# First pass of the attention maximum on 48 rows as two row tiles of the array, with query and key parts stored once

## What is computed

```python
q = shape((xn @ Wq + bq) * SCALING)            # [B*H, L, D], float32
k = shape(xn @ Wk + bk)
attn_weights = einsum('btd,bsd->bts', q, k) + _rel_to_abs(einsum('btd,md->btm', q, rel_k[0]))
attn_probs = softmax(attn_weights, axis=-1)
attn_output = einsum('bts,bsd->btd', attn_probs, v) + einsum('btm,md->btd', _abs_to_rel(attn_probs), rel_v[0])
...
x = x + out_projection(attn_output) + top-2 of 8 experts (xn)
```

## Time and profile before

| | before |
|---|---|
| median of 3 runs | 2135.35 us (2133.4 to 2136.01) |
| the profiled execution, its time | 2129.37 us |
| its span in the profile | 2127.8 us |
| projection and routing | 0 to 194.7 us |
| first pass of group 0, with 8 relative windows | 194.7 to 298 us |
| groups of attention | 298 to about 1190 us |
| experts and combination | about 1190 to 2127.8 us |
| PE, DVE, ACT, POOL busy | 84%, 73%, 51%, 27% |

### The profile page before, as it was taken

How to read it: one execution, slowest core, us unless ns; L and a number is a source line. 1 busy time by engine, 2 the same in 40 slices (tenths; PEclk the granted TensorE clock), 3 DMA queues, 4 the chain that set the end, 5 groups by cost and what they waited for, 6 DMA issues and landing times. The chain is left out here.

```text
span 2127.8 us, 36339 instructions
## 1 busy us (share of the span) xinstructions
PE 1782.1 (84%) x11121; PEld 1025.8 (48%) x11121; DVE 1559.4 (73%) x2621; ACT 1092.2 (51%) x2076; POOL 564.5 (27%) x414
## 2 busy tenths in 40 slices
PE   6992339999999989999888599999999999999920
PEld 4762002333333322333222277777777777788820
DVE  3764787788888878877653298888888888885523
ACT  2541006666666666666878544445444444455500
POOL 1002454233333333300000133323232323320046
PEclk9995559999999999999999799999999999999965
DMA  5998994454444544434551475766666666756535
GB/s 181 341 345 280 261 292 137 123 132 121 134 133 131 137 136 134 114 69 109 161 165 60 173 244 210 250 218 232 219 234 231 222 246 212 253 169 202 168 99 148
DMA packets 214446, 394.97 MB, mean 186 GB/s; under 512 B 16080, under 2 KB 144096, under 8 KB 206176
## 3 DMA queue, kind: packets, MB, share of 16 engines
q1 hardware_dynamic: 189232, 275.33, 42.5%
q0 software_dynamic: 20784, 101.99, 13.9%
q10 hardware_dynamic: 4352, 16.78, 2.2%
HBM read 310.41 MB, written 83.38 MB: 185 GB/s over the span
## 5 line engine op out<-in xcount | busy, mean ns | idle before, releaser
L723 DVE CUSTOM_DVE_ANT_0 t_seen<-t_s,hide 128x1024 bf16<-128x1024 f32 x512 | 604.2, 1221 | 176.8 <-PE t_s L601 176.8
L791 ACT ACTIVATE t_pr<-t_s 128x512 f32<-128x512 f32 x1024 | 560.0, 604 | 285.3 <-PE t_s L614 196.0
L601 PE MATMUL t_s<-t_k,t_q 96*128 96x512 bf16 x1024 | 326.5, 402 | 102.3 <-DVE t_mx L723 78.7
L610 PE MATMUL t_s<-t_q,t_k 98*128 98x512 bf16 x1024 | 362.2, 388 | 51.2 <-ACT t_pr L791 21.6
L1313 ACT ACTIVATE e_sg<-e_pa,e_down 128x256 f32<-128x256 f32 x312 | 148.2, 475 | 421.5 <-PE e_pa L1191 367.3
L1384 DVE SCALAR_TENSOR_TENSOR e_wl<-e_ws,e_up,e_wh 128x512 f16<-128x512 f32 x312 | 319.2, 1035 | 17.1
L1200 PE MATMUL e_py<-e_w2s,e_hT 128*128 128x256 f32 x1248 | 320.7, 380 | 0.0
L610 PEld LDWEIGHTS t_s<-t_q,t_k 98*128 98x128 bf16 x1024 | 97.2, 97 | 387.2 <-ACT t_pr L791 262.9
L625 PE MATMUL t_po<-t_pr,t_vx 128*32 128x512 f32 x2048 | 275.9, 611 | 0.7 <-ACT t_pr L791 0.7
L1191 PE MATMUL e_pa<-e_xh,e_wh 128*128 128x256 f16 x1248 | 239.6, 274 | 43.2 <-DVE e_xl L1376 36.1
L1191 PE MATMUL e_pa<-e_xl,e_wh 128*128 128x256 f16 x1248 | 239.0, 273 | 0.0
(11 more groups left out here) (192 smaller groups left out, 1804.7 us busy)
## 6 DMA issues: line engine op xcount, KB each, us to landing
e_ws<-in_L_ffn_w_dram SPq DMA_DIRECT2D x78, 1024.0 KB, 5.1
e_w2s<-in_L_ffn_w_dram SPq DMA_DIRECT2D x39, 1024.0 KB, 6.2
e_vs<-v_rows POOLq DMA_DIRECT2D x32, 1152.0 KB, 5.8
t_kw<-k_rows POOLq DMA_DIRECT2D x22, 1152.0 KB, 6.9
t_q<-q_stack SPq DMA_DIRECT2D x32, 768.0 KB, 6.0
t_k<-k_stack SPq DMA_DIRECT2D x32, 768.0 KB, 8.8
t_kw<-in_L_ffn_w_dram ACTq DMA_DIRECT2D x16, 1024.0 KB, 4.9
t_kw<-k_rows SPq DMA_DIRECT2D x10, 1152.0 KB, 7.1
```

The costliest lines, as they stand in the source:

```text
L601: last = nc.tensor.matmul(s1[:, buf, half * CH:(half + 1) * CH], q1[0:ROWS, u, h, i * P:(i + 1) * P], k1[0:ROWS, u, h, half * CH:(half + 1 ...
L610: last = nc.tensor.matmul(s2[:, bank, :], k2[0:ROWS + MROWS, u, h, i * P:(i + 1) * P], q2[0:ROWS + MROWS, u, h, half * CH:(half + 1) * CH] ...
L723: nc.vector.tensor_tensor_reduce(out=seen[:, buf, :], in0=s1[:, buf, :], in1=c["hide"][:, (TB - 1 - i) * P:(TB - 1 - i) * P + L], scale=1. ...
L791: nc.scalar.activation(pr[:, k % BP, n % HG], s2[:, turn(u, n)], ACT.Exp).then_inc(exp_ok, 1)
```

## The change

The three bf16 parts are stored once each, and the stacks are built when they are loaded, with one transfer for each 16 rows. The first pass uses only the first three pairs (48 rows): rows 0 to 47 of q1 and k1 for the first 512 keys, rows 64 to 111 for the second 512 keys, each half on its own row tile of the array. k1 then holds 512 keys in each half, and q1 is loaded twice. The second pass keeps its 96 rows.

```diff
-Q_PLACES = ((0, 3, 1), (3, 6, 2), (4, 5, 1))
-K_PLACES = ((2, 5, 1), (1, 6, 4), (0, 1, 1))
+PARTS = 3
+FIRST = 3 * D
+SIDE = P // 2
+Q_PARTS = (1, 0, 0, 0, 1, 2)
+K_PARTS = (0, 1, 0, 2, 1, 0)
...
-        sq=dram("q_stack", [NB, H // HG, HG, ROWS, L], BF16),
-        sk=dram("k_stack", [NB, H // HG, HG, ROWS, L], BF16),
+        sq=dram("q_parts", [PARTS, NB, H // HG, HG, D, L], BF16),
+        sk=dram("k_parts", [PARTS, NB, H // HG, HG, D, L], BF16),
...
-                            rows = stack[b, 2 * k:2 * k + 2, :, :, u * CH:(u + 1) * CH].rearrange(
-                                "g h (d j) c -> (g h d) j c", j=6)
-                            src = part[p][:, a * KC + k, :].rearrange("p (o c) -> p o c", o=1)
-                            sp.dma_start(rows[:, j0:j1:step, :], src.broadcast_to([P, count, CH])).then_inc(st_part[p], 16)
+                            rows = parts[p, b, 2 * k:2 * k + 2, :, :, u * CH:(u + 1) * CH].rearrange("g h d c -> (g h d) c")
+                            sp.dma_start(rows, part[p][:, a * KC + k, :]).then_inc(st_part[p], 16)
...
-        k1 = sb("k1", [P, 2, HG, L], BF16)
+        k1 = sb("k1", [P, 2, HG, CH], BF16)
...
+        N1, N2 = 4 * FIRST // D, 2 * ROWS // D
...
                 def load1(g, u):
-                    for dst, src in ((q1, sq), (k1, sk)):
-                        sp.dma_start(dst[0:ROWS, u], src[g]).then_inc(in1[u], 16)
+                    for half in range(2):
+                        for j in range(FIRST // D):
+                            rows = slice(half * SIDE + j * D, half * SIDE + (j + 1) * D)
+                            sp.dma_start(q1[rows, u], sq[g, Q_PARTS[j]]).then_inc(in1[u], 16)
+                            sp.dma_start(k1[rows, u], sk[g, K_PARTS[j], :, :, half * CH:(half + 1) * CH]).then_inc(in1[u], 16)
 
                 def load2(g, b, gg, u):
-                    for dst, src in ((q2, sq), (k2, sk)):
-                        sp.dma_start(dst[0:ROWS, u], src[g]).then_inc(in2[u], 16)
+                    for dst, src, parts in ((q2, sq, Q_PARTS), (k2, sk, K_PARTS)):
+                        for j in range(ROWS // D):
+                            sp.dma_start(dst[j * D:(j + 1) * D, u], src[g, parts[j]]).then_inc(in2[u], 16)
                     sp.dma_start(vx[:, u], vd[b, gg]).then_inc(vin[u], 16)
...
                     for half in range(2):
-                        last = nc.tensor.matmul(s1[:, buf, half * CH:(half + 1) * CH], q1[0:ROWS, u, h, i * P:(i + 1) * P],
-                                                k1[0:ROWS, u, h, half * CH:(half + 1) * CH], start=True, stop=True)
+                        r = half * SIDE
+                        last = nc.tensor.matmul(s1[:, buf, half * CH:(half + 1) * CH], q1[r:r + FIRST, u, h, i * P:(i + 1) * P],
+                                                k1[r:r + FIRST, u, h, :], start=True, stop=True, tile_position=(r, 0))
```

More of the change, by code:

```diff
@@ L166, in put_part @@
                     sp.wait_ge(part_ok[p], n + 1)
-                    for a, (stack, (j0, j1, step)) in enumerate(((dr["sq"], Q_PLACES[p]), (dr["sk"], K_PLACES[p]))):
-                        count = len(range(j0, j1, step))
+                    for a, parts in enumerate((dr["sq"], dr["sk"])):
                         for k in range(KC):
-                            rows = stack[b, 2 * k:2 * k + 2, :, :, u * CH:(u + 1) * CH].rearrange(
-                                "g h (d j) c -> (g h d) j c", j=6)
-                            src = part[p][:, a * KC + k, :].rearrange("p (o c) -> p o c", o=1)
-                            sp.dma_start(rows[:, j0:j1:step, :], src.broadcast_to([P, count, CH])).then_inc(st_part[p], 16)
+                            rows = parts[p, b, 2 * k:2 * k + 2, :, :, u * CH:(u + 1) * CH].rearrange("g h d c -> (g h d) c")
+                            sp.dma_start(rows, part[p][:, a * KC + k, :]).then_inc(st_part[p], 16)
                 def chunk(n, u, b):
@@ L454, in attention @@
             sem("s2_ok"), sem("exp_ok"), sem("pv_ok"), sem("ot_ok"), sem("otT_ok"), sem("oa_ok"))
-        sq = dr["sq"].rearrange("b g h r c -> (b g) r h c")
-        sk = dr["sk"].rearrange("b g h r c -> (b g) r h c")
+        sq = dr["sq"].rearrange("s b g h d c -> (b g) s d h c")
+        sk = dr["sk"].rearrange("s b g h d c -> (b g) s d h c")
+        N1, N2 = 4 * FIRST // D, 2 * ROWS // D
         vd = dr["vx"].rearrange("(b i p) (g v) -> b g p i v", p=P, i=TB, v=HG * VW)
@@ L643, in group @@
                 def group(g, u, k, more=True, carried=True):
-                    pe.wait_ge(in2[u], 32 * k)
+                    pe.wait_ge(in2[u], 16 * N2 * k)
                     pe.wait_ge(vin[u], 16 * k)
@@ L648, in group @@
                     if more:
-                        pe.wait_ge(in1[1 - u], 32 * (k + u))
+                        pe.wait_ge(in1[1 - u], 16 * N1 * (k + u))
                     done = 0
@@ L668, in _ @@
                 pe.wait_ge(ones_ok, 2)
-                pe.wait_ge(in1[0], 32)
+                pe.wait_ge(in1[0], 16 * N1)
                 for n in range(X1):
```

## The result

The changed kernel takes **2210.68 us** (2200.98 to 2219.36) against 2135.68 us of the kernel before (a fourth run beside the three above moved its median by 0.3): ratio 1.0337, 95% interval 1.0305 to 1.0368, **slower by 75 us**. The profiled execution is 2211.58 us long, its span 2210.1. The forecast was 2175 in a range of 2120 to 2215: the direction is right and the result lies within the range, close to its upper end. Of the 75 us the sum had 40.

What follows compares the result with a forecast made beforehand. Transfers were taken to bound the projection's second half, and PE the groups, with DVE close behind. Terms -7+13+32+10-8 = +40 us on the median 2135.35 gave 2175 us, range 2120 to 2215.

Steps and rivals of the forecast that it cites:

- Stores: Projection: single stores end the transfer limit, -7 us (0 to -9); signs: chunks 17 us apart, DMA share under 1.
- Attention's start: Loads ahead of POOL's window 2 take 32.8 us at 120 GB/s in place of 19.7: +13 us (-1 to +78).
- Group starts: Slower load1 ahead of the copy makes the maxima land 2.6 us later at ten starts: +32 us (+4 to over 200).
- Clock: Behind PE's waits of 3 to 4 us at group starts, six more falls of the clock: +10 us (0 to +17).
- First pass on PE: Row-tile pair costs 0.43 us as today; the 8 pairs before values save 0.10 each: -8 us (-45 to +35).
- the head: The part ahead of the first copy of the maxima, projection and attention's start: -7+13 = +6 us.
- R1: Rival: small loads behind load1 and at attention's start keep up with SP, from about 160 GB/s; 2123 us, chance 0.18.
- R2: Rival: switching between row tiles and whole array is free, pair 0.22 us; 2138 or 2086 us, chance 0.17.
- R3: Rival: each switch on PE waits for the whole way through the array, pair 0.56 us; 2226 us, chance 0.13.
- R4: Rival: the two row-tile halves run one behind the other on PE, pair 0.63 us; 2265 us, chance 0.07.

Runs made afterwards that it cites:

- e2: Kernel before, with only the copy of the maxima issued ahead of load1: 2110.52 us, ratio 0.9925.
- e3: Changed kernel with the copy of the maxima ahead of load1 and the first pass again on 96 rows of the whole array: 2122.57 us, ratio 0.9979.
- e11: Changed kernel, with the copy of the maxima issued from ACT's queue in place of SP's: 2172.18 us, ratio 1.0151.
- e7: Changed kernel, with POOL's second window load of a group held back until load1 has landed: 2165.2 us, ratio 1.0181.
- e9: Kernel before, with load1 in 12 DMAs of all 96 rows (two heads by a third of the columns): 2192.93 us, ratio 1.0300.
- e1: Changed kernel, with only the copy of the maxima issued ahead of load1: 2098.3 us, ratio 0.9864.
- e5: Kernel before with the row tiles, load1 in four DMAs of 48 rows, and the copy of the maxima ahead of load1: 2089.76 us, ratio 0.9811.

## Why the prediction was right in direction and short by half

*Stores, -7.* The signs named came: chunks at 17.0 us, DMA share 0.71, SP's first load 10.4 us earlier, a little more than the end of -9. But the cause, transfers that hold the chunks up, is not borne out: e2 has chunks at 17.0 us with all the stores, e3 and e11 have 20.2 us without them, at a clock of 0.84 and 0.83. That this execution gained its 10 us may be luck with the clock.

*Attention's start, +13.* Half of it: the first copy goes out 3.3 us earlier although the first load did 10 earlier, so +7. POOL's wait grew by 5.2 us, to 20 and not to 28. With the 135 GB/s that the pieces reach alone in place of 120, the same sum gives 3.93 MB in 29.1 us, +9; the last two are not accounted for.

*Group starts, +32: the step that failed.* "at 120 it takes 9.8, and the maxima land 2.6 us later." load1 did take about that (656.06 to 667 and 1026.95 to 1036.4, 135 GB/s alone), and the three starts without a window load, for which the text had a little slack and 2 us each, show 2.9 to 3.2. But at the other starts POOL's window had been left out of the sum. Before, it was issued 4.7 us behind load1's second transfer (639.71 and 635.00) and came through behind load1 and mostly behind the copy; now it is issued as load1's last piece is, and PE waits until it has moved too. The wait became 5.3 to 8.2 us where the text had 3 to 4: over all starts +62.2 us (83.6-21.4) for +32. e7 takes the window away and gets 51.7, e9 has the window's part without the slow rate and gets 64.6: both causes are shown. e1 shows that nearly all of it hangs on the place of the copy.

*Clock, +10: mis-sized.* The price of a fall was taken from one behind a wait of 2.13 us, 1.7. Behind 6.8 us PE works 6.4 at the lower level: 3.2 lost. Taken in 1 us stretches over the groups, half of PE's work at the lower clock is 70.0 us in the changed kernel and 15.9 in the one before, +54; but not all of it lengthens the groups, and e1 still has 29.7. What moving the copy gives beyond the waits is nearer the price: of the 82.8 us more that the place of the copy costs with the change, 59.4 are PE's waits ((83.6-10.4)-(21.4-7.6)), and the remaining +23 are the clock and what hangs on it. That the starts with a long wait would show a fall was right; a few stretches in the middle of groups show one too (17 us from 702), which no term had.

*First pass on PE, -8: about right.* By its own steps the pair was to cost 0.43 and costs 0.41, and the pairs ahead of values were to save 0.10 each and save 0.11: 24*0.02+8*0.11 = 1.4 us a group. An undisturbed group gains 1.9 in e1 against e2, but only ten are undisturbed, and over all 15 the runs give -6.8 (e1 against e2), -10.1 (e1 against e3) and -14.9 (e5 against e2).

Together, groups: 59.4+23.4-6.8 = +76.0 measured, where the sum had 32+10-8 = +34. So the waits were short by some 27 to 30 us and the clock by 13, the row tiles were within a few us, and the head was 9 too high. The sum's miss lies in the start of the groups.

*The rivals.* R1 (small loads keep up with SP) fell: 135 GB/s against the 160 it needed. R2 fell: the pair is not 0.22. R3 fell: it is not 0.56. R4 fell: both tiles in one record of 0.39. The page "SBUF — State Buffer" of the Trainium skill, section "Door 1: The DMA port swizzle", has 104 GB/s for transfers to partitions 0 to 15; the rows show 117 to 144 with several pieces to different rows in flight. By its figure alone the sum would have come nearer (2201), but for a reason that the trace doesn't bear out: the missing time was in what stood beside and behind the loads.

The Trainium skill's page "TensorEngine Tiling (Array Packing)", sections "Overview" and "Key Properties", has a gain of up to 2x and a drain at each change of mode. The trace agrees with both: the two matmuls of a pair run within the 0.39 us of one, and 0.09 on the way in and some 0.10 on the way out give most of the gain back, 0.41 for a pair against 0.43.

## What to carry to other kernels

When a transfer is made slower or its issue longer, look at what is issued behind it and beside it before pricing the transfer itself: here 16 KB of maxima stood behind 1.18 MB that nobody needed for 50 us, and issuing them first was worth 105 us, at least seven times what the row tiles gave in the groups (7 to 15). Cutting a load into pieces is harmless only while nothing urgent shares the engines during the longer issue; a different queue halves the waits here (36.4 us for 83.6) but doesn't give it precedence. And the price of a stall on PE is more than its length: a wait of 7 us cost 3 us more of half-speed work behind it. Before a gain is put down to a change in one stage, the same stage of other variants is worth a look: the projection ran 10 us longer in two traces with the same code.

## What the hardware did that was not expected

- The copy of the maxima got ahead of load1 from no queue: 7.3 us from ACT's queue with load1 in progress, 6.25 from SP's behind it.
- Two loads of 96 rows issued 4.7 us ahead of a 128-row window ran to their end at 250 GB/s, the window at 364 behind them; twelve loads of the same bytes whose issue reached up to the window's ran together with it at 307, and the copy was through only when the window was.
- The work at the lower clock grew with the wait ahead of it, but not in step: 2.9 us of PE's work behind 2.1 us of waiting, 6.4 behind 6.8, and 10.0 in the stretch that begins at the wait of 3.2 us (982 to 992).
- The projection's chunks came 17.0 or 20.2 us apart in traces of the same code, with PE busy throughout and the granted clock at 1.00 or at 0.83 to 0.84.
- The way out of row tiles costs the same into a full-array matmul and into column tiles (0.32 us from start to start in both cases); a full-array matmul of 96 rows ahead of column tiles had cost 0.09 there.
